# Decoder megakernel, two layers: attention projections as f16 pairs, the first norm inside attention, two-pass quantisers, and the convolution's first block on ScalarE and GpSimd

## The reference

```
x = norm(x + attention(x))           # 16 heads of 32, causal softmax
x = norm(x + long_conv(ctx, ctx, x)) # 64 heads of 8: kv = k_i*v_j, causal convolution with a filter of each head, times q
x = norm(x + ffn0(x))                # rms norm, 8-bit activations (one scale), ternary 512x512 weight
x = norm(x + gated_delta_rule(x))    # 512 -> 8192 and 4096, 32 value heads, 256 steps
x = norm(x + decay_scan(x, ctx, ctx))
x = norm(x + ffn1(x))                # 8-bit activations by row, ternary 512->2048->512, silu
```

## Time and profile before

| | us |
|---|---|
| time, median of 3 runs (3673.87 to 3677.07) | 3675.44 |
| time of the profiled execution | 3675.6 |
| its span | 3673.6 |
| attention from the first score matmul to the last added (30.7 to 426.1) | 395.4 |
| norm0 (to the first matmul of the convolution, 445.98) | 19.9 |
| the convolution's loop over heads (459.8 to 692.2) | 232.4 |

### The profile page before, as it was taken

How to read it: one execution, slowest core, us unless ns; L and a number is a source line. 1 busy time by engine, 2 the same in 40 slices (tenths; PEclk the granted TensorE clock), 3 DMA queues, 4 the chain that set the end, 5 groups by cost and what they waited for, 6 DMA issues and landing times. The chain is left out here.

```text
span 3673.6 us, 81792 instructions
## 1 busy us (share of the span) xinstructions
PE 3177.1 (86%) x29389; PEld 2215.0 (60%) x29408; DVE 2612.0 (71%) x4893; ACT 2096.6 (57%) x5396; POOL 1442.7 (39%) x1753
## 2 busy tenths in 40 slices
PE   7999688437999999999999999999999999984185
PEld 5777455225676666666666667666666666762042
DVE  2333499883777777777777777677777777776896
ACT  3333300134767776677766777677776777763453
POOL 1111154103545555455544545445454454530000
PEclk9999899767999999999999999999999999996598
DMA  2000111001010010110101000111001010101201
GB/s 109 12 13 7 77 39 36 26 20 44 13 42 31 25 31 20 42 30 25 31 23 38 30 25 31 26 36 31 24 31 34 28 35 20 31 19 46 92 1 46
DMA packets 43227, 120.67 MB, mean 33 GB/s; under 512 B 5824, under 2 KB 10048, under 8 KB 39488
## 3 DMA queue, kind: packets, MB, share of 16 engines
q1 hardware_dynamic: 42816, 115.30, 9.8%
HBM read 110.75 MB, written 4.54 MB: 31 GB/s over the span
## 5 line engine op out<-in xcount | busy, mean ns | idle before, releaser
L1856 DVE TENSOR_TENSOR delta_Pb<-delta_bank,delta_lev 128x512 f16<-128x512 f32 x448 | 311.1, 694 | 240.0 <-PE delta_bank L2182 240.0
L1848 DVE SCALAR_TENSOR_TENSOR delta_F<-delta_bank,delta_cw,delta_F 128x510 f32<-128x510 f32 (+1 forms) x512 | 381.1, 744 | 66.0 <-ACT delta_far L1667 56.0
L1434 POOL TENSOR_SCALAR_AFFINE_SELECT delta_LA<-delta_LA 128x512 f32<-128x512 f32 x128 | 81.2, 635 | 858.5 <-DVE delta_LA L1877 849.2
L2156 PE MATMUL delta_bank<-delta_xh,delta_qkvh 128*128 128x512 f16 x1024 | 392.3, 383 | 4.5 <-DVE delta_qkvl L1816 3.0
L2156 PE MATMUL delta_bank<-delta_xl,delta_qkvh 128*128 128x512 f16 x1024 | 391.8, 383 | 0.0
L2156 PE MATMUL delta_bank<-delta_xh,delta_qkvl 128*128 128x512 f16 x1024 | 390.7, 382 | 0.0
L1454 POOL TENSOR_TENSOR delta_F<-delta_F,delta_far 128x506 f32<-128x506 f32 x256 | 283.2, 1106 | 256.1 <-DVE delta_F L1848 256.1
L1865 DVE CAST delta_XT<-delta_bank 128x512 f16<-128x512 f32 x448 | 309.7, 691 | 45.4 <-PE delta_bank L2205 45.2
L1661 ACT ACTIVATE delta_F<-delta_bank,delta_cw 128x512 f32<-128x512 f32 x256 | 178.2, 696 | 279.9 <-PE delta_bank L2156 279.7
L1626 ACT ACTIVATE delta_Xi<-delta_bank 128x512 f16<-128x512 f32 x320 | 189.9, 593 | 186.7 <-PE delta_bank L2201 186.7
L2141 PE MATMUL delta_bank<-delta_zh,delta_xh 128*128 128x256 f16 x1024 | 279.7, 273 | 0.6 <-ACT delta_gz L1689 0.6
(11 more groups left out here) (313 smaller groups left out, 9268.5 us busy)
## 6 DMA issues: line engine op xcount, KB each, us to landing
delta_Gb<-g_rows SPq DMA_DIRECT2D x66, 512.0 KB, 5.3
delta_st_qkv<-in_Wqkv SPq DMA_DIRECT2D x17, 1024.0 KB, 8.1
conv_T<-filters SPq DMA_DIRECT2D x32, 256.0 KB, 3.1
delta_st_zo<-in_Wz SPq DMA_DIRECT2D x16, 512.0 KB, 8.4
delta_st_zo<-in_Wout SPq DMA_DIRECT2D x16, 512.0 KB, 6.2
ffn_ahead_W<-in_W SPq DMA_DIRECT2D x2, 4096.0 KB, 17.4
conv_ahead_C<-in_ctx_rev SPq DMA_DIRECT2D x1, 6144.0 KB, 17.7
attn_xt<-in_xT SPq DMA_DIRECT2D x8, 512.0 KB, 3.8
```

Source lines behind the costliest of these rows:

```text
L1848: ve.scalar_tensor_tensor(dst, src, cw_tap(i, 3 - lag), dst, ALU.mult, ALU.add)\
L1856: ve.tensor_tensor(left(Pb[:, lvl, :, :], lvl), comp(bank[5], lvl), bc(lev[:, lvl, :].rearrange("p (n s) -> p n s", s=1 << lvl), 1, 8), AL ...
L2156: ins = te.matmul(bk[:, :], ww[:, QKV[job], kc, :], xx[:, kc, tok:tok + 512], start=(m == 0), stop=(m == 11))
```

## The change

Five parts, in the order of the program.

1. **Projections as f16 pairs.** Weights, times a power of two WS, are split into a high and a low f16 part (ScalarE `weight_high`, VectorE `weight_low`, once for each of four weights), so is each sequence's x^T (`x_high`, `x_low`, 128x1024, once per sequence) and each group's values (`acopy` now writes f16 `ah`, new `alow` on VectorE). A projection is twelve f16 matmuls instead of four f32: high by high, low by high, high by low. `added` becomes a multiply-add. Wo is loaded into Wq's buffer when the low part of Wq is done.
2. **norm0 inside attention.** `norm_stats(n)` on VectorE stands at the front of a slot A, `norm_root(n)` on ScalarE in the slot B after it, `norm_newton(n)` at the front of slot C, `norm_apply(n)` (two passes of 128x512) on ScalarE in slot D before `acopy`. Four slots are added at the end for the last sequence. The stage norm0 is gone, and the load of conv_ahead_C is issued in attention by SyncE.
3. **Convolution.** ScalarE copies bank lo = 0 to SBUF (ys), GpSimd does its three products, VectorE those of lo = 1 to 3. GpSimd's loop begins when the queries are transposed.
4. **norm1** also gives out the mean square of the normalised rows (two small instructions more); ffn0's 16 passes of Square are left out.
5. **Quantisers** in ffn0 and ffn1 take two passes instead of three: (x * scale + MAGIC), then (- MAGIC, min 127).

```
 # attention, TensorE, in use(i): projection i of the order
-                    pe.wait_ge(atc.sem, atc.at(KC * (n + 1)))
-                    for kc in range(KC):
-                        last = te.matmul(ub[:, :], aT[:, kc, c * P:(c + 1) * P], W["o"][:, kc, :],
+                    pe.wait_ge(als.sem, als.at(KC * (n + 1)))
+                    for i in range(3 * KC):
+                        kc = i // 3
+                        aa, ww = ((ah, Wh["o"]), (al, Wh["o"]), (ah, Wl["o"]))[i % 3]
+                        last = te.matmul(ub[:, :], aa[:, kc, c * P:(c + 1) * P], ww[:, kc, :], start=(i == 0),
...
-                    pe.wait_ge(load[n % 2].sem, load[n % 2].at(n // 2 + 1))
+                    pe.wait_ge(xls.sem, xls.at(n + 1))
...
 # attention, ScalarE
+            def x_high(n):
+                act.wait_ge(load[n % 2].sem, load[n % 2].at(n // 2 + 1))
+                if n >= 2:
+                    act.wait_ge(proj.sem, proj.at(10 * (n - 1)))
+                se.activation(flat(x16[:, n % 2, :, :]), flat(xt[:, n % 2, :, :]), ACT.Copy).then_inc(xhs.sem, 1)
...
+            def norm_apply(n):
+                act.wait_ge(newton.sem, newton.at(4 * n + 4))
+                for i in (2 * n, 2 * n + 1):
+                    se.activation(X[:, i, :], X[:, i, :], ACT.Identity, bias=nb[:, i:i + 1], scale=rn[:, i:i + 1])\
+                        .then_inc(normed.sem, 1)
...
+                if s % KC == 1 and s // KC + 1 < B:
+                    x_high(s // KC + 1)
+                if s % KC == 3 and s > KC:
+                    norm_root(s // KC - 1)
+                if s % KC == 1 and s > 2 * KC:
+                    norm_apply(s // KC - 2)
                 if 1 <= s <= GROUPS:
                     acopy(s - 1)
...
 # attention, VectorE
+            def norm_stats(n):
+                for i in (2 * n, 2 * n + 1):
+                    dve.wait_ge(add.sem, add.at(i + 1))
+                    ve.bn_stats(st[:, i, :], X[:, i, :]).then_inc(stats.sem, 1)
+                for i in (2 * n, 2 * n + 1):
+                    dve.wait_ge(stats.sem, stats.at(i + 1))
+                    ve.bn_aggr(mv[:, i, :], st[:, i, :]).then_inc(mom.sem, 1)
...
+            for s in range(GROUPS + 6):
+                if s % KC == 2 and s > KC:
+                    norm_stats(s // KC - 1)
+                if s % KC == 0 and s > KC:
+                    norm_newton(s // KC - 2)
...
                 if 1 <= s <= GROUPS:
                     reciprocals(s - 1)
...
+                if s % KC == 1 and s // KC + 1 < B:
+                    x_low(s // KC + 1)
+                if 1 <= s <= GROUPS:
+                    alow(s - 1)
...
 # convolution, GpSimd, ScalarE, VectorE
+            pool.wait_ge(xc.sem, xc.at(KC * 4))
             with nc.Fori(0, CH // 2, engines=(ENG.Pool,)) as hp:
...
+                    pool.wait_ge(g["yc"].sem, g["yc"].at(1, n1))
+                    pool.wait_ge(g["red"].sem, g["red"].at(2, n0))
...
+                    act.wait_ge(g["mm"].sem, g["mm"].at(1, n1))
+                    act.wait_ge(g["pp"].sem, g["pp"].at(3, n0))
+                    nc.scalar.activation(ys[:, par, :], bank[4 * par][:, 0:PAIRS], ACT.Copy)\
...
-                    for lo in range(KC):
+                    for lo in range(1, KC):
...
-                    dve.wait_ge(g["pr"].sem, g["pr"].at(12, n1))
+                    dve.wait_ge(g["pr"].sem, g["pr"].at(9, n1))
+                    dve.wait_ge(g["pp"].sem, g["pp"].at(3, n1))
...
 # ffn0
-                s_.activation(jk[:, i % 2, :], X[:, i, :], ACT.Square, accum_out=ss[:, i:i + 1])\
...
+            ve.tensor_scalar(v[:, :], square[:, :], 1e-6, None, ALU.add).then_inc(g["v"].sem, 1)
             dve.wait_ge(ahead.loaded["W"].sem, ahead.loaded["W"].at(1))
...
-                ve.tensor_scalar(xn[:, i, :], xn[:, i, :], sc[:, 2:3], 127.0, ALU.mult, ALU.min)\
+                ve.tensor_scalar(xn[:, i, :], xn[:, i, :], sc[:, 2:3], MAGIC, ALU.mult, ALU.add)\
...
-                ve.tensor_scalar(xn[:, i, :], xn[:, i, :], -128.0, MAGIC, ALU.max, ALU.add).then_inc(g["q1"].sem, 1)
```

More of the change, by code:

```diff
@@ L67, with __init__ @@
 class Ahead:
-    def __init__(self, nc, stage, ctx, loads):
+    def __init__(self, nc, stage, ctx, loads, begun=True):
         pt = Parts(nc, stage + "_ahead", ctx)
@@ L73, in __init__, with _, begin @@
         self.loaded = {name: pt.counter(name + "_loaded", 0, 16) for name, _, _ in loads}
[L74 to L78, removed]
+        self.loads = loads
+        if begun:
+            with nc.Block() as block:
+                @block.sync
+                def _(sp):
+                    self.begin(sp)
+    def begin(self, sp):
+        for name, _, src in self.loads:
+            sp.dma_start(self.to[name][:, :, :], src).then_inc(self.loaded[name].sem, 16)
 def make_consts(nc, ctx):
@@ L204, in attn_uses, with attn_stage @@
     return first, slots
-def attn_stage(nc, X, consts, x_dram, xT, WqT, WkT, WvT, WoT):
+def attn_stage(nc, X, consts, ahead, x_dram, xT, WqT, WkT, WvT, WoT):
     with ExitStack() as ctx:
@@ L236, in attn_stage @@
         rec, dgs = counter("recip"), counter("diag")
-        tr, ptc, av, atc = counter("turned"), counter("ptcopy"), counter("values"), counter("acopy")
+        st, mv = sb("st", [P, NT, 6]), sb("mv", [P, NT, 2])
+        var, rn, tn, nb = (sb(n, [P, NT]) for n in ("var", "rn", "tn", "nb"))
+        stats, mom, vars_ = counter("stats"), counter("moments"), counter("variance")
+        ln, root, newton, normed = counter("ln"), counter("root"), counter("newton"), counter("normed")
+        tr, ptc, av = counter("turned"), counter("ptcopy"), counter("values")
+        ahs, als = counter("ahigh"), counter("alow")
+        xhs, xls = counter("xhigh"), counter("xlow")
+        wh = {n: counter("whigh_" + n) for n in "qkvo"}
+        wlo = {n: counter("wlow_" + n) for n in "qkvo"}
         wo, add = counter("wout"), counter("added")
@@ L421, in acopy @@
                 act.wait_ge(av.sem, av.at(j + 1))
-                se.activation(aT[:, j % KC, :], vb[:, 0:S], ACT.Copy).then_inc(atc.sem, 1)
+                se.activation(ah[:, j % KC, :], vb[:, 0:S], ACT.Copy).then_inc(ahs.sem, 1)
+            x_high(0)
+            for n in "qkv":
+                weight_high(n)
             for i in range(4):
@@ L611, in _ @@
                 nc.scalar.activation(dst[:, :, HR:HW], src[:, :, 0:HW - HR], ACT.Copy).then_inc(xc.sem, 1)
+            act.sem_inc(g["yc"].sem, 2 * g["yc"].per)
+            with nc.Fori(0, CH // 2, engines=(ENG.Activation,)) as hp:
+                for par in range(2):
+                    n0, n1 = hp * 2 + par, hp * 2 + par + 2
+                    act.wait_ge(g["mm"].sem, g["mm"].at(1, n1))
+                    act.wait_ge(g["pp"].sem, g["pp"].at(3, n0))
+                    nc.scalar.activation(ys[:, par, :], bank[4 * par][:, 0:PAIRS], ACT.Copy)\
+                        .then_inc(g["yc"].sem, 1)
         @block.vector
@@ L663, with ffn0_stage @@
 MAGIC = 1.5 * 2.0 ** 23
-def ffn0_stage(nc, X, consts, ahead, normw):
+def ffn0_stage(nc, X, consts, ahead, normw, square):
     with ExitStack() as ctx:
@@ L705, in _ @@
             s_ = nc.scalar
[L706 to L711 removed]
+            s_.preload_act_table_set("natural_log_exp_and_others")
             act.wait_ge(g["v"].sem, g["v"].at(1))
@@ L2413, in decoder @@
             ahead = Ahead(nc, "ffn0", nxt, [("W", [P, KC, D], a["W0"])])
-            norm_stage(nc, X, "norm1")
-            ffn0_stage(nc, X, consts, ahead, a["gamma"])
+            square = nxt.enter_context(nc.sbuf_tensor("square", [P, NT], F32))
+            norm_stage(nc, X, "norm1", square=square)
+            ffn0_stage(nc, X, consts, ahead, a["gamma"], square)
         norm_stage(nc, X, "norm2")
```

192 lines of the change are left out of this document (130 added, 62 removed).

## The result

| | before | changed | ratio, 95% interval |
|---|---|---|---|
| median, us | 3674.65 (3671.79 to 3677.07, 4 runs) | 3617.14 (3616.97 to 3619.58, 4 runs) | 0.9845 (0.983 to 0.9859) |

The account below looks back on a forecast made before the run. Attention was taken as bound by TensorE, the convolution by VectorE. Attention with norm0 -7.5, convolution -27.4, norm1 +0.4, ffn0 -10.5 and -6.0, ffn1 -2.5 gave -53.5 on 3675.6: 3622 us, range 3598 to 3642.

Parts of the forecast that it names:

- What TensorE saves, and what the queues give back: Attention: of 6.6 us a period saved on TensorE only 1.4 are left, period 47.3; with norm0 -19.5 if the clock holds.
- The last added: End of attention's slots: the last added comes 5.0 us earlier, before the clock's cost.
- The clock: Attention, slot A: half clock for 3.5 us behind a 3.3 us wait, 1.7 us in each of seven slots, +12.
- The rival in which the clock holds: Attention, slot A: the clock doesn't fall, total -65.5, 3610 us; chance 0.24.
- the one in which the half-clock stretch lasts twice as long: Attention, behind slot A's wait: the slow stretch is doubled, +12, 3634 us; chance 0.16.
- The rival by TensorE's own work: Attention: the queues don't matter, only TensorE's work; attention -52.5, norm0 -14.5, total -113, 3563 us; chance 0.07.
- The convolution: One VectorE block of four goes, 0.92 us a head over 32 heads, VectorE stays the bound: -27.4, bounds -20 and -29.4.
- ffn0: Two parts: head's Newton step no longer waits for the squares, -10.5 us; quantiser loses one pass of three, -6.0.
- ffn1: Quantiser with one pass less: steady loop gains nothing, first and last tiles do, -2.5 us, bounds -1 and -25.
- norm1: Two small instructions more and more waits: +0.4 us.
- the rival in which nothing moves: Whole kernel: attention loses its gains, GpSimd holds the convolution, only ffn0 is left, about 3672 us; chance 0.02.

Follow-up runs that it names:

- e2: The changed kernel with attention's four projections as f32 matmuls again, the first norm still inside attention: 3614.8 us.
- e1: The changed kernel with the first norm taken out of attention and run as its own stage behind it: 3600.0 us.
- e6: The changed kernel with norm_stats and norm_newton behind the maxima, norm_apply behind the values' copy, and x_high and x_low earlier: 3583.6 us.
- e3: The changed kernel with 36 useless bf16 matmuls in each slot A from the second on, during TensorE's wait for the diagonal: 3591.1 us.
- e7: The changed kernel with VectorE's wait for GpSimd's products in the convolution moved from ahead of the reduction to ahead of its own last block: 3612.0 us.
- e9: The changed kernel with 252 useless one-column matmuls at the start of attention, while TensorE waits for the first weights: 3610.1 us.
- e8: The changed kernel with the edits of e6 and e7, and Wo split a slot later: 3575.3 us, ratio 0.9731 to before.
- e12: The kernel before with only the changed kernel's convolution: 3651.8 us against 3670.5, ratio 0.9944.
- e4: The changed kernel with VectorE's norm_stats and norm_newton moved from the front of slots A and C to behind the maxima: 3594.2 us.
- e10: The changed kernel with two blocks of the convolution (0 and 1) on ScalarE and GpSimd, VectorE keeping 2 and 3: 3612.7 us.
- e11: e8 with the 252 one-column matmuls of e9 at the start: 3571.0 us, ratio 0.972 to before.
- e5: The changed kernel with ScalarE's norm_apply moved behind the values' copy, and x_high and x_low earlier: 3595.7 us.

## Why the prediction was right

**What TensorE saves, and what the queues give back.** This step held, and e2, e1 and e6 show it by three ways: f32 projections in its place change nothing, the norm taken out gives 19 us back in attention, the norm left in but reordered 36. The period was forecast at 47.3 and 1.7 for the clock, 49.0; it measured 48.3. Slot C was 0.2 and D 0.15 better than the sum, A 0.3. The term was too small a gain by 4.8 us. The last added came 2.0 later than before, not 7.0 (5.0 earlier, less 12 for the clock): 1.5 of the 5.0 are the clock's, the rest is some 0.5 in each of seven periods (e3, where the clock holds, has 46.7 for 47.3). Behind it 14.3 were saved, as good as the 14.5 forecast.

**The clock.** It fell in six of the seven slots A with the norm's statistics; in the first (from 99.89, 13.55 long, a wait of 2.47) it did not. In the traces of e7 and e9 it fell in that one too. e3 gives the price with all else in place: 10.5 us, forecast 12. By the Trainium skill's rule (TensorE: Matmul & The Clock Gate, "HAM oscillation — how this bites in real kernels"), such a fall is paid in each pass; e3 and the fall in every later period agree. The rival in which the clock holds is out, and so is the one in which the half-clock stretch lasts twice as long: against e3's 14.10 a slot A lost 1.4 to 1.6 us, and one of them (from 290.74) 2.9. The last slot A, which is shorter, lost 1.3 (11.54 for 10.26).

**The rival by TensorE's own work** (3563) is refuted in the changed kernel; e6 and e8 come within 21 and 12 us of it, once the order lets them.

**The convolution** is the term that was mis-sized: 27.4 forecast, 20.8 measured. The mechanism, VectorE rid of one block and still the bound, was right, and GpSimd's products cost 1.5 a head, under the limit of 3.0, and don't slow VectorE's down (its L795 takes 0.62 beside them, as L637 before). Off were two parts: a head saved 0.74, not 0.92, of which 0.11 is the second wait (e7) and some 0.06 a longer jump back of VectorE's loop (0.48 idle for 0.36, every other head; only 0.38 in e2 and e12); and the first reduction came 24.0 us after the first transpose for 22.1, 2.0 lost, not 1.2. Over the 31 steps between the 32 reductions 22.8 were saved, less 2.0 at the start: 20.8.

**ffn0** held to half a microsecond in both parts. **ffn1** gave twice its forecast: VectorE was the bound not in one tile at the start but in three (the reductions of the first three come 7.36 and 8.79 apart, before 9.08 and 9.92, then 10.14 in both kernels). That is 2.9 us; another 2.5 lie at the end, where from the last reduction to the last sum it took 10.9 for 13.4. That the steady loop would gain nothing was right. **norm1** cost 1.3 instead of 0.4, but this stretch isn't steady: with the same norm1 it takes 32.2 in e6 and e9 and 33.1 in the changed kernel, that is 0.4 to 1.3 more than before. What moves it is open, and so is the cause of the 2.1 us between ffn0 and ffn1.

The total came within 4.9 us of the median in part by luck: gains forecast too small in attention and ffn1 (7.8 us), and 2.1 in stages forecast at nothing, stood against one too large in the convolution (6.6).

**Slips that moved no term of the sum.** The kernel before opens slot 0 at 30.73, not 30.3, so the start lost 1.1 where 1.3 were forecast. TensorE has 20 matmul records in a head of the convolution, not 18 (641 in 32 heads), and the convolution has 32 heads of 8, where the comment in the reference above says 64. In the rival in which nothing moves, ffn0's 16.5 us alone would give 3659, not 3672.

## What to carry to other kernels

Before counting what a faster engine saves, write out the in-order queues of the others for one period: work added between two instructions that the fast engine waits for costs time, though its engine is idle half the time (VectorE is busy 183 of attention's 396 us), and the same work two places later costs nothing (3617 became 3584 by order alone). Put new work behind the instruction that another engine waits for next, and look at the granted clock behind each wait that is left. Where an instruction has to wait for the one just ahead of it, put its other waits further up, ahead of one that doesn't.

## What had not been expected of the hardware

**Code ahead of a loop changes what its jump back costs.** TensorE runs the delta rule as a loop whose jumps lie some 455 us apart, and at each it has two waits that the profile puts to issue. The first of the four jumps in TensorE's timeline, in the kernel before:

```profile
1438.00 0.34 PE L2182 MATMUL delta_bank<-delta_Xi,delta_Lt 128*128 128x64 f16 x6 [1.51 <-issue]
1441.08 0.29 PE L2182 MATMUL delta_bank<-delta_Xi,delta_Lt 128*128 128x64 f16 x2 [2.74 <-issue]
```

In the changed kernel:

```profile
1389.05 0.40 PE L2326 MATMUL delta_bank<-delta_Xi,delta_Lt 128*128 128x64 f16 x8 [1.21 <-issue]
1392.23 1.01 PE L2384 MATMUL delta_bank<-delta_F 128*128 128x256 f32 x2 [2.78 <-issue]
```

In e3:

```profile
1378.51 0.41 PE L2329 MATMUL delta_bank<-delta_Xi,delta_Lt 128*128 128x64 f16 x8 [1.24 <-issue]
...
1381.61 0.38 PE L2297 MATMUL delta_bank<-delta_oh,delta_ch 128*128 128x512 f16 x1 [1.10 <-issue]
```

In e9:

```profile
1387.71 0.40 PE L2328 MATMUL delta_bank<-delta_Xi,delta_Lt 128*128 128x64 f16 x8 [1.62 <-issue]
...
1391.09 0.38 PE L2296 MATMUL delta_bank<-delta_oh,delta_ch 128*128 128x512 f16 x1 [2.03 <-issue]
```

The second wait stands at another instruction in each, L2384 in the changed kernel, and at delta_oh in e3 and e9, and takes 2.78, 1.10 and 2.03. From the delta rule's last transpose of X to ffn1's first maximum the changed kernel takes 2628.4, e3 2612.5, e9 2620.5, with the same instructions. These two stand apart: in e1, e2, e4 to e8 and e10 the stretch takes 2627.3 to 2629.1. The first waits of the four jumps lie 456 to 457 us apart in the changed kernel, 452 to 453 in e3, 454 to 456 in e9.

That 252 instructions more ahead of the loop move the waits is shown by e9, with half of e3's 16 us; the same 252 in e11 gave 3.1 against e8. That it is the place of the loop's code through which they act is argued and not shown; why they give 16, 8 or 3 us, and what would place the loop best, is open.

**The clock after a wait.** Waits of TensorE for the diagonal of 1.40 (e4), 1.62 (e5) and once 2.47 us (slot at 99.89) left the granted clock at 1.0; one of 3.01 was followed by 3.5 us at 0.56, and before, one of 2.17 at the poorly filled end of attention by 0.50. Even the same wait in the same slot goes either way. Behind the 2.47 us of the first slot A with the norm, in the changed kernel and in e9:

```profile
105.90:109.40 3.50, 3.50 (x31) 3.37 (x32) 1.38 (x2) 3.44 (x17) 0.00 (x0) 1.00 0.00 0
```

```profile
105.90:109.40 3.50, 3.50 (x18) 3.48 (x19) 0.69 (x1) 3.31 (x16) 0.00 (x0) 0.54 0.00 0
```

That slot A takes 13.55 in the one and 15.09 in the other. So neither the length of a wait nor its place in the slot says whether the clock falls; what does isn't shown here.
